# A two-layer transformer block on one core: the fourth score of each key tile is issued behind the value products of the tile before it

## What is computed

```
x = x + _L0_xattn_ref(_layernorm(x), ctx_512, W_k, b_k, ln_gamma, ln_beta)   # bilinear scores, layer norm, softmax
x = x + _L0_ffn_ref(_layernorm(x), w_gate, w_up, w_down)                     # Hadamard rotation, 8-bit tokens, ternary weights
x = x + _L1_xattn_ref(_layernorm(x), ctx_512, ctx_512)                       # 32 query heads, 8 key heads, head size 16
x = x + _L1_ffn_ref(_layernorm(x), gate_w, w0, w1, wo, ...)                  # 8 experts, the 2 best of each token
```

```
scores  = jnp.einsum('bkgsd,bktd->bkgst', qh, kh) / scale
weights = jax.nn.softmax(scores, axis=-1)
out     = jnp.einsum('bkgst,bktd->bkgsd', weights, vh)
```

## Time and profile before

| | us |
|---|---|
| runs (3) | 1666.21, 1669.02, 1674.38 |
| span of the profiled execution, first to last instruction | 1670.3 |
| TensorE busy (MATMUL) | 1567.2 (94%) |
| VectorE busy | 948.0 (57%) |
| ScalarE busy | 717.6 (43%) |
| GpSimd busy | 702.1 (42%) |
| the reductions R (L2057), 248 of 1220 ns | 291.3 |
| the exponentials E (L1420), 512 of 601 ns | 271.7 |
| mean granted TensorE clock, as a share of full speed | 0.975 |

### The profile page before, as it was taken

One profiled execution on the slowest core, in us unless ns is written; L12 is line 12 of the kernel. 1 busy time (PEld: TensorE's weight loads), 2 busy tenths in 40 slices (PEclk: granted clock), 3 DMA queues, 4 the chain that ended last, 5 costly groups with the idle time before them and its releaser, 6 DMA issues.

```text
span 1670.3 us, 24439 instructions
## 1 busy us (share of the span) xinstructions
PE 1567.2 (94%) x8124; PEld 1047.5 (63%) x8150; DVE 948.0 (57%) x1539; ACT 717.6 (43%) x1160; POOL 702.1 (42%) x479
## 2 busy tenths in 40 slices
PE   6869999999889999999899899999999999999998
PEld 4555657565543434434333778788788888788886
DVE  6998979796878897887885622222122222222221
ACT  5885646455547777777677211111111111111111
POOL 1124251633513125254354765670862180930064
PEclk9889999999898999999999999999999999999999
DMA  9189800000231445243430625231440140530088
GB/s 357 56 305 386 291 1 1 0 1 1 84 94 47 123 132 149 82 126 111 148 114 28 224 70 189 82 120 32 182 176 26 59 155 26 188 127 26 26 140 213
DMA packets 90944, 196.16 MB, mean 117 GB/s; under 512 B 7153, under 2 KB 9074, under 8 KB 90226
## 3 DMA queue, kind: packets, MB, share of 16 engines
q1 hardware_dynamic: 71746, 156.68, 28.2%
q0 software_dynamic: 7168, 17.04, 4.5%
q10 hardware_dynamic: 11952, 21.43, 3.9%
HBM read 113.28 MB, written 81.32 MB: 117 GB/s over the span
## 4 chain that ended last, share of the span: by engine, by line
PE 68%; DVE 16%; POOL 6%; ACT 4%; issue 3%; DMA 3%; another core or an unknown queue 0%; SPq 0%; POOLq 0%; DVEq 0%; ACTq 0%
PE psum L2929 11%; PE psum L2931 11%; PE psum L2930 11%; PE psum L2580 6%; DVE neg_max L2057 5%; PE psum L2782 5%; PE psum L2771 5%; PE psum L2744 4%; POOL expert_weight_parts L1052 3%; PE psum L2625 3%; PE psum L2595 2%; DMA w_of_even_expert<-in_L_ffn_w 2%; PE psum L2953 2%; POOL expert_weight_parts L1051 1%; DVE inner_rotated_t_second L1926 1%
## 5 line engine op out<-in xcount | busy, mean ns | idle before, releaser
L2057 DVE TENSOR_REDUCE neg_max<-psum 128x2 f32<-128x1024 f32 x248 | 291.3, 1220 | 49.5 <-PE psum L2744 48.3
L1420 ACT ACTIVATE probabilities<-psum 128x512 f32<-128x512 f32 x512 | 271.7, 601 | 85.2 <-PE psum L2771 81.3
L2199 DVE TENSOR_TENSOR expert_inner<-psum,expert_inner 128x512 f32<-128x512 f32 x78 | 53.9, 692 | 388.7 <-ACT expert_inner L1526 378.6
L2929 PE MATMUL psum<-expert_weight_parts,sorted_tokens_t_first 128*128 x624 | 250.8, 402 | 8.8 <-POOL expert_weight_parts L1052 5.1
L2930 PE MATMUL psum<-expert_weight_parts,sorted_tokens_t_first 128*128 x624 | 246.8, 396 | 0.0
L2931 PE MATMUL psum<-expert_weight_parts,sorted_tokens_t_second 128*128 x624 | 246.8, 395 | 0.0
L1526 ACT ACTIVATE expert_inner<-psum 128x512 f32<-128x512 f32 x78 | 46.7, 599 | 396.7 <-PE psum L2931 396.7
L2771 PE MATMUL psum<-query_rows,key_rows 50*128 50x512 f32 x512 | 179.3, 444 | 4.1 <-ACT probabilities L1420 3.0
L2744 PE MATMUL psum<-key_rows,query_rows 48*128 48x512 f32 x496 | 170.6, 491 | 11.7 <-DVE neg_max L2057 5.8
L2929 PEld LDWEIGHTS psum<-expert_weight_parts,sorted_tokens_t_first 128*128 128x128 f32 x624 | 117.7, 189 | 37.4 <-issue 11.1
L2782 PE MATMUL psum<-probabilities,value_and_one 128*32 128x512 f32 x1024 | 140.3, 620 | 0.8 <-ACT probabilities L1420 0.7
(11 more groups left out here) (316 smaller groups left out, 2924.3 us busy)
## 6 DMA issues: line engine op xcount, KB each, us to landing
sorted_x<-zero_rows SPq DMA_DIRECT2D x9, 3960.0 KB, 30.5
w_of_odd_expert<-in_L_ffn_w SPq DMA_DIRECT2D x8, 2048.0 KB
wo_of_expert<-in_L_ffn_wo SPq DMA_DIRECT2D x7, 2048.0 KB, 8.6
query_rows<-query_rows_of_units SPq DMA_DIRECT2D x64, 192.0 KB, 3.5
w_of_even_expert<-in_L_ffn_w SPq DMA_DIRECT2D x6, 2048.0 KB, 11.6
sorted_tokens<-sorted_x ACTq DMA_DIRECT2D x39, 264.0 KB, 2.8
sorted_y<-expert_out ACTq DMA_DIRECT2D x39, 256.0 KB
query_rows_of_units<-dims_first SPq DMA_DIRECT2D x32, 256.0 KB
```

What stands on the lines that cost most here:

```text
L1420: nc.scalar.activation(prob[t % 2][:, i * SEQ:(i + 1) * SEQ], bank[4 + n % 3], ACT.Exp, scale=HD ** -0.5).then_inc(c_e, 1)
L2057: nc.vector.tensor_reduce(of_pair[:, p, st, :], ring(("max", (m, i))).rearrange("p (h n) -> p h n", h=2), AX.X, ALU.max, negate=True).then ...
L2199: nc.vector.tensor_tensor(h, bank[2 * half + 1], h, ALU.mult).then_inc(e_h, 1)
L2929: nc.tensor.matmul(out_bank, hi[:, cols], w_r[:, bass.ds(w_at, 512)], start=start, stop=False)
```

## The change

In units 0 to 29 the order on TensorE becomes S0 M0 S1 M1 S2 M2 M3 V S3, with the extra jobs behind S3. The halves of the maxima change places: M0 now has h = 0, M1 has h = 1, M2 has h = 0 and M3 has h = 1. M0 and M2 are now in the same row half as the score ahead of them (S0, S2), and so is M1 with S1. In units 30 and 31 the order S0 S1 S2 V S3 stays as it was; in unit -1 only the halves change. Nothing else of the program is touched: the same instructions, the same waits, the same banks and ring places, and no change on the other engines.

```
             def attention(u):
                 for t in range(ST):
-                    for p in range(2):
-                        for h in range(2):
-                            if there(u):
-                                if p == 1 and h == 1 and not there(u + 2):
-                                    attend(ST * u + t - 1)
-                                score(u, t, p, h)
-                            if there(u + 2):
-                                maximum(u + 2, 2 * t + p, 1 - h, h == 0)
+                    for i in range(4):
+                        if there(u) and i < 3:
+                            score(u, t, i // 2, i % 2)
+                        if there(u + 2):
+                            maximum(u + 2, 2 * t + i // 2, i % 2, i % 2 == 0)
                     k = ST * u + t - 1
-                    if 0 <= k < ST * UNITS and (there(u) and there(u + 2) or not there(u) and t == 0):
+                    if 0 <= k < ST * UNITS and (there(u) or t == 0):
                         attend(k)
+                    if there(u):
+                        score(u, t, 1, 1)
                     if t == 0 and u >= 0 and there(u + 1):
                         neg_max_transposed(u + 1)
```

## The result

| | before | change |
|---|---|---|
| median of the runs, us | 1669.66 | 1685.45 |
| lowest to highest, us | 1666.21 to 1674.38 (10 runs) | 1674.60 to 1745.49 (10 runs) |
| ratio, 95% interval | | 1.0056 (1.0036 to 1.0075) |
| ScalarE idle before L1420, us | 85.2 | 117.6 (177.2 in the slower profile) |
| VectorE idle before L2057, us | 49.5 | 45.3 (81.8) |

The change makes the kernel slower by some 9 us (6 to 12.5 by the interval: 1669.7 x 0.0036 and x 0.0075). The ratio leaves out four of the change's ten executions, of 1701 to 1745 us at a mean granted clock of 0.927 to 0.957, and with them the median of all ten is 16 us above before and not 9.

The account below looks back on a forecast made before the run. Phase c was taken as bound by loops of waits between tiles, with no engine full. Eleven units without a chunk (+5.4) and 13 with one (+3.1), routing 0, gave +8.5 us on 1669.0: 1677.5, range 1663 to 1688 (the forecast's own 1668 to 1682).

Parts of the forecast that it names:

- The loop of the plain tile: Tile without extra jobs, V to next V: 2.84 to 2.95 us, taken as 2.89, against 2.61 before.
- the middle term: In the plain tile's new loop: M2 runs behind S2 in the same row half, 0.34 us.
- The unit: Growth of one unit of phase c: +0.49 us without a chunk (11.88 after 11.39), +0.24 with one.
- the negated maxima: Tile with their transposition (t = 0), V to next tile's first reduction: 2.65 us after 2.42, bounds 2.42 and 2.7.
- Attended and chunk tiles: Tiles with attended values or a chunk: stay at 3.28 us, set by the ring of maxima; TensorE's 3.14 leaves 0.14 cover.
- The rival in which S3 ahead of a full-array job costs more: Chance 0.15: S3 between V and a full-array job costs 0.2 to 0.3 us beyond 0.43; total 1687.5 us.
- The halves: Row halves of the maxima: changing them costs nothing by itself, four matmuls deep on both sides before and after.
- Routing tiles: Tiles with eight transpositions: V 0.57 us earlier, partly taken back; six routing units counted as 0, bounds -3 and +2.
- The sum: Units 0 to 29: 11 x 0.49 plus 13 x 0.24, together +8.5 us, giving 1677.5.
- ScalarE's idle time: ScalarE's idle time before line L1420, in the profile after the change: stays near 85 us.
- The clock: Rival, chance 0.07: more TensorE idling before S2 lowers the clock once in each of 11 plain units; +22 us, 1700.
- the fast rival: Chance 0.14: S2 and M2 are no serial step, plain tile stays at 2.61, other tiles gain; 1655.5 us.

Follow-up runs that it names:

- E3: As a run: the change with S2 moved behind M2 and M3, 1674.0 us, ratio 1.0084 (the same label also names an exponential).
- E8: The change with M2 and M3 moved behind V and S3, ahead of the extra jobs: 1726.9 us, ratio 1.0340.
- E1: The change's order alone, with the maxima keeping the row halves of the kernel before: 1674.5 us, ratio 1.0063.
- E2: The kernel before with only the row halves of the maxima changed, order kept: 1693.2 us, ratio 1.0175.
- second profile: Profile of a later execution of the same changed kernel, the one read for comparing single tiles: span 1672.4 us.
- E10: The change with a stall (first reduction of unit 4, t = 0, made five times): 1706.6 us, ratio 1.0253.
- E4: The kernel before with only M3 put ahead of S3: 1664.0 us, ratio 1.0010.
- E9: The kernel before with a stall (first reduction of unit 4, t = 0, made five times): 1677.9 us, ratio 1.0058.
- first profile: Profile of the changed kernel that fell in one of its long executions: span 1734.6 us.
- E12: The kernel before with only the row halves of the maxima changed, plus the same stall: 1701.5 us, ratio 1.0204.

## Why the prediction was right, step by step

**The loop of the plain tile: right.** 2.84 to 2.95 was given, and 2.84 came, with E3 as the exponential that ends S2's wait. Its three terms stand in the trace: V to S2 2.17 (560.82 to 562.99) for 2.18, S2 to the second maximum 0.33 for 0.34, and that to V 0.33 of 0.32 to 0.43. I took 2.89; the lower end was the right one, since the two maxima follow S2 closely, as in the stream of the earlier trace rows. E3 and E8 show the middle term by taking it out.

**The unit: right in the sum, three terms off.** +0.47 came for +0.49 without a chunk, and +0.23 for +0.24 with one. But from V to the first reduction behind the negated maxima 2.65 was given and 2.46 came (566.50 to 568.96), 0.19 less, and the two plain tiles are 0.10 less than the 5.78 taken. Against that V stands 0.43 behind the reduction where the unit begins (560.39 to 560.82), and not 0.17, 0.26 more: I had taken S3 out from ahead of V and left out that M2 and M3 still follow S2 there. The three nearly cancel, which is luck: 0.43 + 5.68 + 2.46 + 3.28 is 11.85, for 11.88.

**Attended and chunk tiles: right.** 3.32 and 3.20 came for 3.28. The rival in which S3 ahead of a full-array job costs more needed 0.1 more on all of them and 0.25 on the negated maxima; S3 to the job is 0.43 (567.57 to 568.00), as in the earlier trace rows. "TensorEngine Tiling (Array Packing)" of the Trainium skill, Key Properties, by which a change of mode drains the array, adds nothing beyond that 0.43 here.

**The halves: right for the change, wrong as a statement.** "Four deep on both sides either way" counts the matmuls in each half and not who is beside whom behind a wait. In the new order it makes no difference (E1). In the old one it costs some 20 us (29 with the executions at a lower mean clock, E2), more than the whole change.

**Routing tiles: the gain was sized at 0 and is about 1.2.** V came 0.43 behind M2 for 0.35, and the pair of units 12 and 13 is 0.41 shorter, that of 20 and 21 0.39; three such pairs are -1.2. It lay within the bound of -3.

**The sum: near the measured time, and in part by luck.** 11 x 0.47 + 13 x 0.23 = 8.2, less 1.2 is 7, for the forecast 8.5; the ratio gives 9 (6 to 12.5). The second profile's span, 1672.4, is 10.4 above the median span of before on its chip, 1662.0. But the two kinds of unit don't hold for all 24. Unit by unit, the shortest in four profiles of the new order (the change's two, E1 and E10) against the shortest in three of the loop of before (before, E4 and E9), about half follow them (+0.45 to +0.50 and +0.20 to +0.23), but units 10 and 17 lose nothing, 15 and 23, with the ranks, are 0.34 shorter, and unit 29 is 0.82 longer. Units 1 to 29 together come to +5.0, so by this estimate some 5 of the 9 us are in the tiles. The rest is not located. Stalls and the clock are the candidates: unit 26 took 14.8 to 18.0 in three of the four profiles of the new order and 12.2 to 13.9 in the three others.

**ScalarE's idle time: wrong.** "Near 85 us" came as 117.6. The copies out of PSUM show where it was before. Rows of the groups by line in phase c (busy us and mean ns, then idle before); before, then the change:

```profile
L1404 ACT ACTIVATE dims_of_tokens<-psum 128x512 f32<-128x512 f32 x15 | 9.0, 598 | 10.6 <-PE psum L2732 10.6
L1467 ACT ACTIVATE normed_t_of_batch<-psum 128x1024 f32<-128x1024 f32 x6 | 6.2, 1026 | 9.6 <-PE psum L2834 9.6
```

```profile
L1404 ACT ACTIVATE dims_of_tokens<-psum 128x512 f32<-128x512 f32 x15 | 9.0, 598 | 0.2
L1467 ACT ACTIVATE normed_t_of_batch<-psum 128x1024 f32<-128x1024 f32 x6 | 6.2, 1025 | 4.3 <-PE psum L2833 4.3
```

With L1410 (6.9 to 0.0) and the three small ones of the routing (8.5 to 4.0) the copies waited 35.6 us before and 8.5 after: E3, late now, waits instead of the copy behind it. All of ScalarE's waiting there went from 120.8 to 126.1, 5 us more. So the idle time before one line was a poor indicator; the sum over ScalarE, or the 0.72 before E3 in each plain tile (0.6 to 0.7 had been given), was the good one.

**The clock: named at 0.07, with the wrong mechanism.** I let it fall once in each plain unit through 0.3 us of idle time, for 22 us. The second profile shows that this doesn't happen: its granted clock is 1.00 from 560 to 838 us, over some twenty units. What happens is that a fall which something else causes can last: the one at the start of phase c 119 us in the first profile, and the one behind the stall by hand 27 us for 7 (E10 and E9). While it lasts a plain tile loses 1.65 us (4.49 for 2.84) where the loop of 2.61 loses 1.46 (4.07 in E8). The execution of the first profile is 62 us longer than that of the second. The forecast of 1677.5 is right for the executions that the ratio compares (1669.7 x 1.0056 = 1679.0); the median of all, 1685.45, carries what I had left at 7 in 100.

"TensorE: Matmul & The Clock Gate" of the Trainium skill, A second HAM failure mode, says that a loop which cycles through PSUM banks can idle for short times between groups of matmuls often enough to make the clock swing between its levels. The order with S2 behind E3 could be such a loop (0.23 of idle time before S2 in each plain tile), and E10 stays low longer than E9. But E12, with a plain tile of the same length, doesn't; the clock stayed at 1.00 from 560 to 838 us with these waits in it; and in the stretch at 1.2 GHz the records show no idle time at all, 25.00 busy of 25.00. No run here shows the rule at work.

## What to carry to other kernels

Moving an instruction out of one loop of waits puts it into another: write down the new loop to its end, with every neighbour that shares the row half of the array, before counting what the old one loses. An order of row halves is only right or wrong together with the place of the waits; change both or price both. And price a loop at both clock levels, since a tile that depends on more steps of TensorE in series loses more whenever the clock is low (1.65 us for 1.46 here).

## What the runs showed of the hardware

- Matmuls of different row halves do not always start in the order of the program. Of the two matmuls behind S2 in the loop shown above, the record that carries M3's signal to VectorE starts at 562.998, 0.006 behind S2; M2, which stands ahead of M3 in the program and shares S2's half, starts at 563.333. In the stretch at 1.2 GHz it is 539.490 for M3 and 540.074 for M2. "TensorE: Matmul & The Clock Gate" of the Trainium skill, The mechanism (Part 3), which I used against the fast rival, says that matmuls keep program order in start and end; for the starts this trace differs. The conclusion stood, since M2, in one half with S2, started 0.34 behind it.
- Two matmuls of 512 columns in one half start 0.33 to 0.34 apart after a wait and 0.23 in a stream; in different halves, 0.00 to 0.01 (562.992 and 562.998). At 1.2 GHz the first is 0.59.
- TensorE's share of busy time doesn't tell its clock: 25.00 of 25.00 at 0.50, with 91 records, and 24.25 of 25.00 at 1.00, with 149.
- From one stall of 4 to 4.5 us on, the lower clock lasted 7 us in one order of the same matmuls and 27 us in another, in one profile of each.
